# The 50 trips of a written-out loop become hardware loops of two trips: a graph layer with 30 feed-forward steps on one core

## The chip, the core and the metric

One core of a Trainium2 chip. The metric is the device time of one execution in microseconds (us). The kernel uses all engines: TensorE (PE; PEld is its weight load), VectorE (DVE), ScalarE (ACT), GpSimd (POOL) and SyncE (SP), which issues most DMAs.

## The reference

There are 12500 nodes of 256 features and 200000 edges sorted by destination.

```python
xn = _layernorm(x)
support = xn @ gnn_weight
gnn  = relu(segment_sum(support[src] * edge_weight[:, None], dst))
mix  = attention_linear(xn)                # 4 heads, k and v normed, kv summed over all nodes, then wo, bo
x1 = x + gnn + mix
h = _layernorm(x1)
for _ in range(30):                        # lax.scan
    h = h + 0.01 * tanh(h)
    h = h * sigmoid(h)
    h = layernorm(h, ln_w, ln_b)
    h = h @ W.T + b
out = x1 + h
```

## The kernel before

The rows are cut into 100 tiles of 125 rows. There are three stages. Stage A norms x into `xn_d`. Stage B (the `b_trip` function of each engine, 10 passes of 10 tiles, most of them in a hardware loop, `Fori`) sums the attention's kv matrix, and aggregates the messages of the first tiles. Stage F is the rest, and the longest: the 30 feed-forward steps.

Stage F has 5 rounds (`ROUNDS`) of 20 tiles. A round has 10 trips (`TRIPS`), and a trip has 15 slots (`SLOTS`). A slot is one feed-forward step of four tiles, a quad; five quads (`QUADS`) take turns, so a trip is three steps of all five. In a slot PE transposes the next quad (`f_transpose`, L1357 in `quad_transpose`) and multiplies the present one (`f_multiply`, L1365 in `quad_multiply`). ACT does tanh (L747), silu (L757), copies the transposed rows (L770) and norms two or three tiles (L762). DVE does the sum after tanh (L1139), the statistics (L1107, L1112), the shift (L1117) and the low part of a split product (`f_low`, L1152). POOL computes the reciprocal deviation (L494) and norms a tile (L581).

Twelve of 15 slots split the product in three matmuls of a faster type (24 matmuls); the others use 16 slower ones. In rounds 0 to 3 the trips also carry the work of the next round's 20 tiles (flags `g` and `xx` of `f_trip`): POOL gathers source rows (L529, 17 chunks of 128 edges a tile), DVE builds a matrix for each chunk (`hot`, L991), PE sums them (`AGG`, L1252, after a wait for `hot_ready` in L1249), and a few matmuls, copies and loads follow (XB). The last round has none of this, and all 15 slots are split.

Each engine runs its own program. The order of the work is the order in which `f_trip` emits it; engines meet only in semaphores. Every wait in stage F is against a count that follows from the trip number `t`, the round `r` or the trip within the round `u`, as in

```python
n = t * SLOTS + s
pe.wait_ge(S("normed"), n + 1)
pe.wait_ge(S("hot_ready"), j * KC + (c + 1))
```

Before the change `trips_of_f` calls the body 50 times in Python. So each of the 50 trips stands in the program of each engine as its own instructions, and all these counts are constants. In stage B, where the trips are in a `Fori`, the counts are worked out in registers while the program runs, on the engine's own sequencer, and PE's loop starts after one written-out pass.

Of the kernel before, what the change touches and what calls it, by code (L numbers as in the profile page):

```python
# [23 lines left out]
ROUNDS = TILES // ROUND  # L24
SLOTS = 3 * QUADS
TRIPS = STEPS // 3
# [4 lines left out]
LAST_G = G_TRIPS // TRIPS  # L31
# [72 lines left out]
def build(nc, x, src, dst, ew, w_gnn, wq, wk_t, wv_t, wo_t, bo, gk, bk, gv, bv, ln_w, ln_b, wf_t, bf, out):  # L104
# [14 lines left out]
    with ctx:  # L119
# [169 lines left out]
        def trips_of_f(eng, body):  # L289


            for r in range(ROUNDS):
                more = r < ROUNDS - 1
                for u in range(TRIPS):
                    end = u == TRIPS - 1
                    body(r * TRIPS + u, u % 2, r, u, end, more and not (end and r == LAST_G), more, not more and end)

        def splits(t, s, xx):

# [10 lines left out]
        def _(sp):  # L310
# [131 lines left out]
            def f_trip(t, h, r, u, end, g, xx, last):  # L442
# [18 lines left out]
                if end:  # L461
                    for q in range(QUADS):
                        out_store(r, q)

            trips_of_f(sp, f_trip)
            sp.wait_ge(S("out_stored"), 32 * QUADS * ROUNDS)
            sp.wait_ge(S("edges_loaded0"), 48 * (TILES // 2 + 1))
# [4 lines left out]
        def _(pool):  # L472
# [117 lines left out]
            def f_trip(t, h, r, u, end, g, xx, last):  # L590
                for s in range(SLOTS):
# [22 lines left out]
                    if not (last and s + 3 >= SLOTS):  # L614
                        f_rstd(n + 3, (s + 3) % QUADS)

            trips_of_f(pool, f_trip)


        @block.scalar  # L620
        def _(act):
# [165 lines left out]
            def f_trip(t, h, r, u, end, g, xx, last):  # L787
                for s in range(SLOTS):
# [31 lines left out]
                    if g and s == A_TAIL + 2:  # L820
                        g_relu(t * 2 + EARLY_G, xb_use(t, 3))

            trips_of_f(act, f_trip)


# [655 lines left out]
```

## Time and profile before

| what | value |
|---|---|
| time before, median of 3 runs | 4650.79 us (4643.75 to 4659.26) |
| the profiled execution: its own time, its span | 4659.26 us, 4657.4 us |
| PE busy over the span, matmuls | 4163.1 us (89%), 28680 |
| PE weight loads | 3764.2 us (81%), 28680 |
| DVE, ACT, POOL busy | 80%, 76%, 69% |
| instruction fetch, q8 and q14 | 229 packets, 3.75 MB; 165 packets, 1.35 MB |
| granted TensorE clock, mean | 0.976 |

The span runs from the first to the last instruction. A share is a mean over all stages. Stage F fills about four fifths of the span. Instructions of the sequencer (waits, register operations, branches) do not count as busy; they stand in the trace under the engine's name with a q.

### The profile page before, as it was taken

Reading aid. Unit: us, or ns where it says so; the run is one execution under the profiler, and the core shown is the slowest. Engines: PE = TensorE matmul, PEld = TensorE weight load, DVE = VectorE, ACT = ScalarE, POOL = GpSimd, SP = SyncE. Lnnn points to the kernel's source line nnn. Section 1 sums busy time; section 2 is a strip of 40 time slices with the busy share of each in tenths; the row PEclk is TensorE's granted clock in tenths of the full one; section 3 lists DMA queues with packets and bytes.
Section 4 is the critical chain, followed back from the end, with each engine's and each line's share of the span. In section 5 each row is a group of like instructions: output and inputs, shape, how many; then the busy total and the mean of one; then the engine's idle time right before and its main releaser. Section 6 shows DMA issues by size and latency. Waiting matters only on the chain.

```text
span 4657.4 us, 86661 instructions
## 1 busy us (share of the span) xinstructions
PE 4163.1 (89%) x28680; PEld 3764.2 (81%) x28680; DVE 3741.5 (80%) x7288; ACT 3522.3 (76%) x5199; POOL 3219.2 (69%) x3713
## 2 busy tenths in 40 slices
PE   0377777799999999999999999999999999888888
PEld 0244544699999999999999999999999999888888
DVE  4355555688888898888898888889888888888888
ACT  3212211588888888888888888888888889888887
POOL 2445555588888888888888888888888886444444
PEclk9698999899999999999999999999999999999999
DMA  6433333222222232222232222223222221100000
GB/s 202 129 104 105 108 99 107 71 77 77 77 72 77 77 99 72 77 77 77 72 94 82 78 71 78 76 78 93 77 77 78 72 78 54 45 1 1 1 1 23
DMA packets 229800, 351.47 MB, mean 75 GB/s; under 512 B 78161, under 2 KB 168382, under 8 KB 229406
## 3 DMA queue, kind: packets, MB, share of 16 engines
q0 software_dynamic: 82496, 224.47, 16.5%
q1 hardware_dynamic: 142873, 117.94, 8.8%
q8 instruction: 229, 3.75, 0.3%
q10 hardware_dynamic: 4037, 3.95, 0.3%
q14 instruction: 165, 1.35, 0.1%
HBM read 307.30 MB, written 38.91 MB: 74 GB/s over the span
## 4 chain that ended last, share of the span: by engine, by line
PE 65%; DVE 17%; issue 5%; ACT 4%; another core or an unknown queue 4%; POOL 2%; DMA 2%; DVEq 0%; SPq 0%; ACTq 0%; POOLq 0%
PE MM L1365 36%; PE AGG L1252 11%; PE TR L1357 11%; DVE st L1107 4%; DVE T L1139 4%; DVE v_low L1152 4%; PE XB L1264 3%; ACT T L747 3%; PE MM L1288 1%; DVE hot L991 1%; POOL gat L529 1%; DVE k_ss L1008 1%; DVE sh L1117 1%; PE XB L1258 1%
## 5 line engine op out<-in xcount | busy, mean ns | idle before, releaser
L529 POOL DMA_INDIRECT gat<-xn_d,src_cur x1700 | 1691.2, 995 | 685.3 <-issue 443.7
L1365 PE MATMUL MM<-w_high,v_high 128*125 128x256 f32 x5040 | 1464.4, 291 | 0.0
L1365 PE MATMUL MM<-w_low,v_high 128*125 128x256 f32 x5040 | 1416.8, 281 | 0.0
L1365 PE MATMUL MM<-w_high,v_low 128*125 128x256 f32 x5040 | 1415.8, 281 | 0.0
L1139 DVE SCALAR_TENSOR_TENSOR T<-T,MM 125x1024 f32<-125x1024 f32 x725 | 884.4, 1220 | 406.8 <-ACT T L747 403.4
L762 ACT ACTIVATE T<-T,sh,rs 125x256 f32<-125x256 f32 x2102 | 1109.7, 594 | 32.5 <-DVE sh L1117 29.3
L1107 DVE BATCH_NORM_STATS2 st<-T 125x6 f32<-125x512 f32 x1500 | 989.4, 701 | 1.1 <-ACT T L757 1.0
L1252 PE MATMUL AGG<-gat,hot 128*125 128x256 f32 x3400 | 865.4, 386 | 127.4 <-DVE hot L991 65.0
L494 POOL TENSOR_TENSOR rs<-ve,minus_half 125x4 f32<-125x4 f32 x755 | 783.7, 1038 | 230.2 <-DVE ve L1112 218.3
L1365 PEld LDWEIGHTS MM<-w_high,v_high 128*125 128x125 f32 x5040 | 938.8, 186 | 0.0
L1365 PEld LDWEIGHTS MM<-w_low,v_high 128*125 128x125 f32 x5040 | 936.2, 186 | 0.0
L1365 PEld LDWEIGHTS MM<-w_high,v_low 128*125 128x125 f32 x5040 | 935.7, 186 | 0.0
L747 ACT ACTIVATE T<-MM 125x1024 f32<-125x1024 f32 x725 | 740.7, 1022 | 229.2 <-PE MM L1365 226.2
L1357 PE MATMUL TR<-ident,T 125*128 125x125 f32 x6040 | 782.3, 272 | 143.5 <-DVE v_low L1152 118.5
L1357 PEld LDWEIGHTS TR<-ident,T 125*128 125x128 f32 x6040 | 680.9, 141 | 256.1 <-DVE v_low L1152 175.3
L1252 PEld LDWEIGHTS AGG<-gat,hot 128*125 128x125 f32 x3400 | 614.0, 190 | 260.3 <-issue 120.1
L757 ACT ACTIVATE T<-T 125x1024 f32<-125x1024 f32 x750 | 789.5, 1053 | 0.0
L581 POOL TENSOR_SCALAR T<-T,rs,sh 125x256 f32<-125x256 f32 x898 | 499.6, 559 | 374.8 <-DVE sh L1117 355.3
L1152 DVE SCALAR_TENSOR_TENSOR v_low<-TR,v_high 128x1000 fp32r<-128x1000 f32 x630 | 750.2, 1191 | 2.2 <-ACT v_high L770 2.2
L770 ACT ACTIVATE v_high<-TR 128x1000 fp32r<-128x1000 f32 x630 | 631.9, 1003 | 78.7 <-PE TR L1357 62.6
L991 DVE TENSOR_SCALAR hot<-iota_f,d_loc,w_loc 128x125 f32<-128x125 f32 x1700 | 506.0, 349 | 0.0
L1365 PE MATMUL MM<-w_plus,v_full 128*125 128x256 f32 x1920 | 434.3, 379 | 0.0
(176 smaller groups left out, 2963.3 us busy)
## 6 DMA issues: line engine op xcount, KB each, us to landing
gat<-xn_d,src_cur POOLq DMA_INDIRECT x1700
k_x<-xn_d SPq DMA_DIRECT2D x100, 125.0 KB
g_u<-gen_d SPq DMA_DIRECT2D x100, 125.0 KB
g_x<-in_x SPq DMA_DIRECT2D x100, 125.0 KB
a_x<-in_x SPq DMA_DIRECT2D x24, 512.0 KB, 5.5
xn_d<-a_n SPq DMA_DIRECT2D x24, 512.0 KB, 3.9
x_cur<-x_d SPq DMA_DIRECT2D x25, 448.0 KB
out_rows<-x_cur SPq DMA_DIRECT2D x25, 448.0 KB
```

The lines of the kernel that those rows point to most:

```text
L494: pool.tensor_tensor(out_, var, minus_half[0:p, 0:n], ALU.pow).then_inc(S(done), 1)
L529: pool.indirect_dma_start(gat[c][:], None, xn_d, bass.IndirectOffsetOnAxis(ap=src_cur[e][:, c:c + 1], axis=0)).then_inc(S(f"gathered{c}"), 16)
L747: nc.scalar.activation(lane(T, q), product(b), ACT.Tanh).then_inc(S("tanh_done"), 1)
L757: nc.scalar.activation(lane(T, q), lane(T, q), ACT.Silu).then_inc(S("silu_done"), 1)
L762: last = nc.scalar.activation(T[0:R, q * QT + t, :], T[0:R, q * QT + t, :], ACT.Identity, bias=sh[q][0:R, t:t + 1], scale=rs[q][0:R, t:t + 1])
L770: nc.scalar.activation((v_high if split else v_full)[b][:], TR[:, :, 0:4 * R], ACT.Copy, bias=1.0).then_inc(S("transposed_copied"), 1)
L1107: last = v.bn_stats(st[q][0:R, t:t + 2].rearrange("p t k -> p (t k)"), rows_[:, t:t + 2, :].rearrange("p t f -> p f t"))
L1139: v.scalar_tensor_tensor(out=lane(T, q), in0=lane(T, q), scalar=0.01, in1=h, op0=ALU.mult, op1=ALU.add).then_inc(S("u_done"), 1)
L1152: v.scalar_tensor_tensor(out=v_low[b][:], in0=TR[:, :, 0:4 * R], scalar=1.0, in1=v_high[b][:], op0=ALU.add, op1=ALU.subtract).then_inc(S(" ...
L1252: mm(AGG[0:R, 0:D], hot[c][:], gat[c][:], start=c == 0, stop=c == KC - 1).then_inc(S("chunks_multiplied"), 1)
L1357: last = tp(TR[:, t // 2, at:at + R], T[0:R, q * QT + t, h * 128:(h + 1) * 128], ident[0:R, 0:R])
L1365: last = mm(MM[b][0:R, t // 2, t % 2 * D:(t % 2 + 1) * D], rows_, w, start=k == 0, stop=k == len(products) - 1)
```

## The change

The 50 calls become loops of the hardware (`Fori`) whose body is two trips, with the tenth pair of each round behind the loop, because the last trip of a round has other flags. Rounds 0 to 2 stand in an outer loop; rounds 3 and 4 are written out, each with its own inner loop. Each inner loop runs four times. So 12 trips stand in the program instead of 50, and `t`, `u` and (in the first nest) `r` are values in registers. The work, its order, and every count that is waited for are the same.

```diff
-            for r in range(ROUNDS):
+            with eng.Fori(0, LAST_G) as r:
+                with eng.Fori(0, TRIPS // 2 - 1) as u:
+                    for h in range(2):
+                        body(r * TRIPS + u * 2 + h, h, r, u * 2 + h, False, True, True, False)
+                for h in range(2):
+                    body(r * TRIPS + (TRIPS - 2 + h), h, r, TRIPS - 2 + h, h == 1, True, True, False)
+            for r in range(LAST_G, ROUNDS):
                 more = r < ROUNDS - 1
-                for u in range(TRIPS):
-                    end = u == TRIPS - 1
-                    body(r * TRIPS + u, u % 2, r, u, end, more and not (end and r == LAST_G), more, not more and end)
+                with eng.Fori(0, TRIPS // 2 - 1) as u:
+                    for h in range(2):
+                        body(u * 2 + (r * TRIPS + h), h, r, u * 2 + h, False, more, more, False)
+                for h in range(2):
+                    body(r * TRIPS + TRIPS - 2 + h, h, r, TRIPS - 2 + h, h == 1, more and h == 0, more, not more and h == 1)
```

`LAST_G` is 3, `TRIPS` is 10, `ROUNDS` is 5. The arguments of `body` are `t, h, r, u, end, g, xx, last`.

## Rows read from the trace of the kernel before

**Rows 1.** The page: busy us (share) and instructions; fetch queues: packets, MB.
```profile
PE 4163.1 (89%) x28680; PEld 3764.2 (81%) x28680; DVE 3741.5 (80%) x7288; ACT 3522.3 (76%) x5199; POOL 3219.2 (69%) x3713
...
q8 instruction: 229, 3.75, 0.3%
...
q14 instruction: 165, 1.35, 0.1%
```

**Rows 2.** Windows: stretch, us; PE, PEld, DVE, ACT, POOL busy; clock; DMA share; GB/s.
```profile
2125.50:2280.40 154.90, 153.08 (x1098) 143.52 (x1097) 136.03 (x266) 137.17 (x201) 126.61 (x144) 1.00 0.27 76
4250.80:4384.50 133.70, 117.68 (x963) 111.48 (x964) 114.16 (x180) 116.17 (x152) 62.95 (x90) 1.00 0.00 1
```

**Rows 3.** Chain of the last round, in order: start us, us, what.
```profile
4255.94 2.86 PE MM L1365 x24
...
4264.85 2.86 PE MM L1365 x24
```

**Rows 4.** One line's instructions, stage B's loops, 250 to 760 us; ns min/median/max.
```profile
L1323 PEldq COMPARE_BRANCH  x8: 83/215/238, 317.3 to 751.9; - x8
...
L1249 PEldq ALU_OP  x256: 32/32/32, 262.8 to 745.8; - x128
...
L990 DVEq ALU_OP  x272: 40/40/40, 261.9 to 744.4; - x136
```

**Rows 5.** DVE timeline, in stage B's loop and in stage F: start us, us.
```profile
304.91 1.36 DVE L991 TENSOR_SCALAR hot<-iota_f,d_loc,w_loc 128x125 f32<-128x125 f32 x5
...
1022.36 0.85 DVE L991 TENSOR_SCALAR hot<-iota_f,d_loc,w_loc 128x125 f32<-128x125 f32 x3
```

**Rows 6.** PE timeline across a back edge of stage B's loop.
```profile
317.21 2.07 PE L1264 MATMUL XB<-w_agg,xb_t 128*125 128x256 f32 x4 [6.43 <-ACT xb_t L671]
319.07 0.62 PE L1280 MATMUL TR<-ident,k_x 125*128 125x125 f32 x2
```

**Rows 7.** DMA queues, 250 to 750 us, then 1018 to 1020 us.
```profile
q8 instruction: 1, 0.02, 0.0%
...
q8 instruction: 1, 0.02, 3.0%
```

**Rows 8.** Line L514's group, and DMA issues: KB each, us to landing.
```profile
L514 POOL DMA_INDIRECT u_g<-xn_d,u_src x1 | 1.3, 1293 | 9.6 <-DMA u_row<-in_dst 9.6
...
lnb_c<-in_ln_b ACTq DMA_DIRECT2D x2, 0.5 KB, 5.4
...
u_g<-xn_d,u_src POOLq DMA_INDIRECT x1, 4.1
```

**Rows 9.** PE around a trip's end: L1249, the chain, PE's timeline.
```profile
L1249 PEldq EVENT_SEMAPHORE  x2: 51/51/51, 2282.2 to 2282.4; - x2
...
2285.32 0.85 PE TR L1357 x8
...
2290.37 0.81 PE L1357 MATMUL TR<-ident,T 125*128 125x125 f32 x6
```

**Rows 10.** DVE timeline across the same trip's end.
```profile
2285.55 1.22 DVE L1139 SCALAR_TENSOR_TENSOR T<-T,MM 125x1024 f32<-125x1024 f32 x1 [0.34 <-ACT T L747]
...
2286.76 1.32 DVE L1107 BATCH_NORM_STATS2 st<-T 125x6 f32<-125x512 f32 x2
...
2288.20 1.19 DVE L1152 SCALAR_TENSOR_TENSOR v_low<-TR,v_high 128x1000 fp32r<-128x1000 f32 x1
```

**Rows 11.** PE timeline after two pauses of stage B, then windows.
```profile
286.88 1.99 PE L1252 MATMUL AGG<-gat,hot 128*125 128x256 f32 x8 [2.47 <-issue]
...
351.67 3.78 PE L1252 MATMUL AGG<-gat,hot 128*125 128x256 f32 x8 [3.20 <-issue]
...
351.67:355.30 3.63, 3.63 (x9) 2.86 (x10) 1.37 (x4) 1.16 (x4) 0.86 (x1) 0.50 0.15 46
```

**Rows 12.** Waits, 1740 to 3900 us: who for whom, us, times, longest us.
```profile
POOL gat L529 <- issue: 243.3, 906, 2.1
...
PEld TR L1357 <- issue: 5.4, 9, 1.3
```

## The prediction

> **What bounds the kernel now.** I read the page first, then windows of whole trips, the chain, and the instructions around one trip's end. The page gives the means [rows 1]; the windows show that they hide two regimes. Two trips of rounds 0 to 3 take 154.90 us, 77.45 a trip, and PE is busy 153.08 us of them [rows 2]: PE is the bound, with 1% to spare. In the last round two trips take 133.70 us, 66.85 a trip, and PE is busy 117.68 of them [rows 2]. There a ring of waits sets the pace: from one batch of 24 matmuls to the one two slots later the chain takes 4264.85 - 4255.94 = 8.91 us [rows 3], 4.45 a slot, and 15 slots are 66.8 us. In both regimes no time is spent on branches or fetches that any row of stage F shows, apart from small waits put down to issue [rows 12].
>
> **What the change adds and removes.** No matmul, transfer or count changes. Removed are 38 of 50 trips from the program. Added are three things.
>
> *Registers.* Counts that were constants are computed. Stage B does this already. PE has 256 register operations of 32 ns for the waits of L1249 in eight passes, and DVE 272 of 40 ns for 136 chunks, two each [rows 4]. Yet five hot matrices take 1.36 us in that loop and three take 0.85 us in stage F [rows 5]: with 0.34 us for one (an operation outlasts its turn), both are 0.255 us each. So DVE's register work runs under the operation before it. In stage F most DVE and ACT operations are longer than a hot, and PE's sequencer is far ahead (next paragraph). I cost this at nothing; its cover is the operation that runs meanwhile. From above: if two 40 ns operations stayed in the open in each of 750 slots it would be 60 us. The hot rows are nearest, so zero.
>
> *The branches themselves.* A compare-and-branch of PE takes 0.215 us [rows 4]; across a back edge of stage B the transposes start at 319.07 while the matmuls before them end at 319.28 [rows 6]. Nothing is lost there.
>
> *The code at the branch's target.* This is the term that decides. In 250 to 750 us, with PE seven times round its loop of one pass, one packet of instructions came on q8 [rows 7]: a body that small stays with the engine. The new bodies are larger. Two trips are 1098 + 1097 = 2195 matmuls and weight loads [rows 2], without waits and register work. q8 carried 3.75 MB for 57,360 of them [rows 1], 65 bytes each, so a body is over 140 KB, five or more times stage B's. No row shows a branch back over so much. I take it that the code at the loop's head is gone by then, and that PE stops until it has come. DVE, ACT and POOL (266, 201 and 144 operations [rows 2]) may stop too, more likely DVE.
>
> The Trainium skill's page "Runtime: NRT & Kernel Launch" (section on instruction fetch mechanics) says that a taken branch to code outside the engine's small store, 128 KiB on PE and 32 KiB elsewhere, waits for a DMA fetch. It speaks against this change: by it PE, with 140 KB and more, misses at every back edge and the sum is the one below; were only the small loops of the trace to go by, the body might as well stay and the sum would be nothing. No run shows yet which holds.
>
> How long is a miss, L? From below it is the packet alone: 3.0% of 16 engines in 2 us, 0.96 us for 16 KB [rows 7]. From above it is a transfer of 0.5 KB that stood behind others, 5.4 us from issue to landing [rows 8]. Nearest is the single gather of L514: 4.1 us to landing, of which POOL spent 1.3 writing it [rows 8], so 2.8 us, and a fetch's packet is 0.96 longer: L = 3.7 us.
>
> What is covered? At the end of the trip at 2280 PE's sequencer passed its last wait for a chunk at 2282.4, and PE reached the next transposes at 2285.32 [rows 9]: it had 2.9 us of matmuls ahead. From these I take off 0.8 us, by choice, for the loop's register work and the waits behind the branch (32 and 51 ns each [rows 4, 9], with gaps between them): 2.1 us of cover. DVE's side gives the same. Its branch can be passed once the sum of 2285.55 is released; the next statistics start at 2286.76, 1.2 us later; and the low part that follows ends at 2289.39, 0.98 us before the transposes at 2290.37 that need it [rows 9, 10]: 2.2 us. The two run side by side, so the longer counts, not both. A back edge costs L - 2.1 = 1.6 us. PE has 1% to spare, so nothing is caught up.
>
> There are 15 taken back edges of inner loops and 2 of the outer. In rounds 0 to 3 that is 12 + 2 = 14: 14 x 1.6 = 22.4 us. In the last round there are 3; PE idles 0.5 us a slot there, and DVE's body is a third shorter and may stay: L - 2.4 = 1.3 us, 3.9 us. SP misses at outer edges at most, and its loads are issued far ahead: nothing.
>
> Sum: 22.4 + 3.9 = 26.3; for what two or three engines that miss together add to each other I put 3 us more, by choice. 29 us on the profiled execution's 4659.26 is 4688; that one was the slowest of three, 0.2% over the median, so from 4650.79 I forecast **4680 us**, +0.6%.
>
> At the bounds: L = 0.96 costs nothing; L = 5.4 costs 14 x 3.3 + 3 x 3.0 = 55 us. A pause of 2.47 us left PE fast (8 matmuls in 1.99 us); after one of 3.20 us the same 8 took 3.78, and the windows show the clock at 0.50, the 1.2 GHz level [rows 11]. So at L = 5.4 each edge would also pay up to 1.8 us, 31 more: 4737.
>
> **Rivals.**
>
> *Nothing happens* (27%). The code stays, or the fetch comes in the shade of the 2.9 us that PE is ahead. For it: the small loops, and the cover of over 2 us. It decides at L below 2.9 us (14 x 0.8 = 11 us, under 0.3%). Time: 4645 to 4664, most likely 4651.
>
> *The registers are in the open* (10%). Each slot pays 0.08 us on the path, because PE's bound leaves no slack: 60 us besides the 29, 4740. Against it: rows 5. For it: the last round's ring runs through small DVE operations (shift, variance), where there is less to hide under.
>
> *Faster* (6%). Straight code makes the engines fetch 229 and 165 packets [rows 1]; if loops of ACT, POOL and SP stay, part of that traffic is gone, and with it the waits put down to issue at PE's transposes: 5.4 us in 2160 us [rows 12], some 10 us over stage F. POOL's 243.3 us over 906 gathers are 0.27 us each [rows 12], a regular gap that no fetch explains, so I leave them out. 4641 us.
>
> **How the numbers follow.** The forecast (misses that cost 0.8 to 3.3 us an edge) has 57%; its own range is 4664 to 4737. What a measurement tells from no change is about 0.3%, 14 us. Slower: 57 + 10 = 67%. Same: 27%. Faster: 6%. The range from 4643 to 4735 leaves out the worst of the registers, the end of the clock's case and the end of the fast side, some 2 in 10 together.
>
> **What the new profile would show.** PE pauses of 1 to 2 us every 155 us, put down to issue or to an engine that paused itself, and trips between them at 77.5 us; q8 still above 220 packets, as each pass is fetched anew, and q14 below 165 if some bodies stay. If the trips between the edges are longer than 77.5, the registers are the cause. If q8 falls to some 60 packets, the body stays and the forecast's first step is wrong. I would be wrong above all in L, and in how far misses of several engines add up instead of lying side by side.

## The result, and the profile after

| | median us (lowest to highest) | runs |
|---|---|---|
| before | 4644.23 (4629.45 to 4659.26) | 7 |
| after | 4691.23 (4666.44 to 4700.16) | 7 |

The ratio is 1.0089, with a 95% interval of 1.0064 to 1.0114: slower by 47 us between the medians and by 41 by the ratio, whose interval is 30 to 53 us. The profiled execution of after took 4715.59 us (span 4713.7), above all the timed ones. It entered stage F 17.5 us later than the profiled execution of before, behind code that the change does not touch. So stage F is compared by itself: from the start of ACT's tanh of slot 4 (slots counted from 0) in the first trip to the same one of the last trip. It took 3702.7 us before and 3741.4 after, **+38.7 us**. The trace holds 50 such starts, 15 slots apart, and each trip's length is a difference of two of them.

The page of after, to be held against [rows 1]; then one group of its fifth part, and its chain:

```profile
PE 4175.6 (89%) x28680; PEld 3781.5 (80%) x28680; DVE 3741.3 (79%) x7288; ACT 3523.1 (75%) x5199; POOL 3232.2 (69%) x3713
...
q8 instruction: 263, 4.31, 0.4%
...
q14 instruction: 215, 1.76, 0.1%
...
PE 65%; DVE 15%; issue 8%; ACT 4%; another core or an unknown queue 3%; POOL 3%; DMA 2%; DVEq 0%; ACTq 0%; SPq 0%; POOLq 0%
...
L1115 DVE BATCH_NORM_STATS2 st<-T 125x6 f32<-125x512 f32 x1500 | 989.9, 702 | 28.8 <-issue 27.9
```

The program shrank to 12 trips, yet both fetch queues carry more packets than before (229 and 165): each pass fetches its code anew. "Issue" is 8% of the chain. DVE sat idle 27.9 us for it before its statistics, 2 us for each of the 14 edges of rounds 0 to 3.

PE's branches, by line: L292 is the outer loop, L293 the inner loop in it, L300 the inner loops of rounds 3 and 4 (ns min/median/max, then first and last start). Last, the list of PE's waits (us in total, times, longest):

```profile
L292 PEldq COMPARE_BRANCH  x3: 79/4164/5327, 1684.4 to 3258.6; - x3
...
L293 PEldq COMPARE_BRANCH  x12: 83/3828/4582, 1058.0 to 3103.5; - x12
...
L300 PEldq COMPARE_BRANCH  x8: 83/3504/4252, 3414.2 to 4575.0; - x8
...
PE TR L1365 <- issue: 32.3, 16, 3.5
```

A branch that falls through takes 0.08 us. A taken one takes about 4 us, and that is the miss: PE's sequencer stands in the branch until its target has come. PE's transposes then waited for issue in 16 places, 32.3 us together; before, no such wait stands in the list for this line. The waits are shorter than the branches because PE had matmuls queued. The chain at one edge shows how much (start us, us, what):

```profile
1214.52 2.86 PE MM L1373 x24
1217.38 0.86 PE AGG L1260 x4
1218.24 1.93 issue
1220.17 1.05 PE TR L1365 x8
```

The branch began at 1215.68 and ended at 1219.54. PE's queued matmuls ran out at 1218.24, 2.56 us after its start. From the branch's end to the transposes at 1220.17 are another 0.63 us of register work and waits. So the cover was 2.56 - 0.63 = 1.93 us, and the pause 1.93.

The clock is the second part. Windows behind three edges (stretch, us; PE, PEld, DVE, ACT, POOL busy; clock; DMA share; GB/s), and the chain across the third and the second of them:

```profile
1220.20:1223.00 2.80, 2.80 (x25) 2.80 (x26) 1.41 (x3) 1.75 (x3) 2.22 (x3) 1.00 0.25 61
1690.50:1692.40 1.90, 1.87 (x9) 1.90 (x10) 0.00 (x0) 0.00 (x0) 1.06 (x1) 0.50 1.03 314
...
3421.00:3423.50 2.50, 2.50 (x15) 2.50 (x13) 2.44 (x6) 1.52 (x4) 1.38 (x2) 0.53 0.00 0
```
```profile
3416.79 2.17 issue
3418.97 1.05 PE TR L1365 x8
3420.01 4.37 PE MM L1373 x24
```
```profile
1687.01 3.52 issue
1690.53 1.90 PE TR L1365 x8
1692.43 4.58 PE MM L1373 x24
```

After a pause of 1.93 us PE went on at 1.00, the 2.4 GHz level. After one of 3.52 us it ran at 0.50, the 1.2 GHz level: 8 transposes and 24 matmuls took 6.48 us instead of 3.91, 2.6 us lost besides the pause. After one of 2.17 us the drop came late, and cost 4.37 - 2.86 = 1.5 us. By the starts of matmuls two other edges (1850, 4174 us) lost some 1.5 us each in this way. Together the clock is about 7 of the 38.7 us. The length of the pause alone does not decide it: after 2.58 us, the longest pause at an inner edge (1060.6), PE went on at full speed, and after 2.05 us, at 4172.3, it did not.

### The profile page after: what moved, and what is told of

Read it like the earlier page. It is cut to its first block, busy times and chain, and to the rows that moved or that the text cites. A ratio compares the mean times of both kernels' runs of the same rounds, so it can differ in the third digit from the quotient of the medians.

```text
span 4713.7 us, 94631 instructions
## 1 busy us (share of the span) xinstructions
PE 4175.6 (89%) x28680; PEld 3781.5 (80%) x28680; DVE 3741.3 (79%) x7288; ACT 3523.1 (75%) x5199; POOL 3232.2 (69%) x3713
## 4 chain that ended last, share of the span: by engine, by line
PE 65%; DVE 15%; issue 8%; ACT 4%; another core or an unknown queue 3%; POOL 3%; DMA 2%; DVEq 0%; ACTq 0%; SPq 0%; POOLq 0%
PE MM L1373 35%; PE AGG L1260 12%; PE TR L1365 11%; DVE st L1115 4%; DVE T L1147 4%; PE XB L1272 3%; DVE v_low L1160 3%; ACT T L755 3%; PE MM L1296 2%; POOL gat L537 2%; DVE hot L999 1%; PE XB L1266 1%; DMA a_x<-in_x 1%; DVE sh L1125 1%
## 5 line engine op out<-in xcount | busy, mean ns | idle before, releaser
L1115 DVE BATCH_NORM_STATS2 st<-T 125x6 f32<-125x512 f32 x1500 | 989.9, 702 | 28.8 <-issue 27.9
L1260 PE MATMUL AGG<-gat,hot 128*125 128x256 f32 x3400 | 876.8, 390 | 136.5 <-DVE hot L999 74.2
```

The lines of the kernel that those rows point to most:

```text
L1115: last = v.bn_stats(st[q][0:R, t:t + 2].rearrange("p t k -> p (t k)"), rows_[:, t:t + 2, :].rearrange("p t f -> p f t"))
L1260: mm(AGG[0:R, 0:D], hot[c][:], gat[c][:], start=c == 0, stop=c == KC - 1).then_inc(S("chunks_multiplied"), 1)
```

## The experiments

All change `trips_of_f` only. Kernels of one group shared the runs of before: e1 to e4 with 4652.37 us (18 runs), e5 to e8 with 4660.93 (23), e9 to e12 with 4651.65 (17). F is the extra length of stage F in the one profiled execution of each, in us over before's 3702.7. In the columns after it, F is taken apart by trips, each against the same trip of before: the 12 trips that begin at a taken inner edge in rounds 0 to 3; the two outer edges, each with the two trips before and the two behind it; the last round. What is missing, under 3 us, lies elsewhere. F is one execution's. It stands up to 8 us from the difference of the medians and up to 12 from the ratio, so differences of a few us between two kernels are read from edges and trips, not from F.

| kernel | median us | ratio (95%) | F | inner | outer | last |
|---|---|---|---|---|---|---|
| after | 4691.23 | 1.0089 (1.0064 to 1.0114) | +38.7 | 25.8 | 7.6 | 5.2 |
| e1 hints on all loops | 4672.31 | 1.0041 (1.0026 to 1.0055) | +13.5 | -3.9 | 14.2 | 1.4 |
| e2 outer loop only | 4659.31 | 1.0011 (0.9999 to 1.0024) | +6.8 | -1.7 | 9.3 | -0.2 |
| e3 PE alone loops | 4695.28 | 1.0082 (1.0068 to 1.0095) | +40.7 | 26.0 | 7.4 | 7.1 |
| e4 the four others loop | 4673.44 | 1.0033 (1.0021 to 1.0046) | +20.2 | 11.4 | 8.2 | -0.1 |
| e5 inner loops only | 4692.41 | 1.0089 (1.0065 to 1.0113) | +36.4 | 28.8 | -0.1 | 7.0 |
| e6 the same, with hints | 4668.00 | 1.0024 (1.0009 to 1.0040) | +3.4 | -3.3 | 1.5 | 2.9 |
| e7 DVE alone loops | 4678.37 | 1.0041 (1.0025 to 1.0058) | +20.9 | 14.5 | 8.3 | 0.0 |
| e8 POOL alone loops | 4674.71 | 1.0031 (1.0015 to 1.0046) | +16.9 | 10.3 | 6.3 | -0.2 |
| e9 hints on PE alone | 4676.34 | 1.0048 (1.0030 to 1.0067) | +22.5 | 14.0 | 7.3 | 1.3 |
| e10 hints on the others | 4706.43 | 1.0125 (1.0106 to 1.0143) | +47.1 | 23.8 | 17.0 | 3.7 |
| e11 four trips a pass | 4672.42 | 1.0059 (1.0037 to 1.0080) | +15.8 | 6.7 (4 edges) | 7.9 | 2.9 |
| e12 ACT alone loops | 4649.65 | 1.0001 (0.9986 to 1.0016) | +1.5 | 0.0 | 1.5 | -0.1 |

### e1: a branch hint on every loop

```diff
+            def loop(n):
+                return nc.Fori(0, n, engines=OrderedEngineSet([eng.engine]), hint_back_edge=True)
-                with eng.Fori(0, TRIPS // 2 - 1) as u:
+                with loop(TRIPS // 2 - 1) as u:
```

The same stands for the outer loop. In the trace it is one more instruction on each engine, at the head of each pass; PE's, for the outer and the inner loop:

```profile
L296 PEldq BRANCH_PREFETCH_HINT  x3: 45/45/55, 873.8 to 2443.4; - x3
L297 PEldq BRANCH_PREFETCH_HINT  x12: 31/36/36, 874.1 to 2909.7; - x12
```

> All loops of stage F on all engines announce their back edge at the head of each pass, so that the code at the loop's head can be fetched while the pass runs. Nothing else differs from the changed kernel; the registers and branches stay. Theory 1 (missing code at the branch): PE's taken branches fall from about 4 us to under 0.5 us, and the time comes back to the kernel before within 0.2% (up to 10 us over it). Theory 2 (register work in the open): the time stays about 40 us (0.9%) over the kernel before. Theory 3 (the nest of loops disturbs something else, such as the order of loads): it stays too, and PE's branches are short.

PE's branches in e1, outer and inner loop; its waits; and DVE's chain at the first outer edge:

```profile
L296 PEldq COMPARE_BRANCH  x3: 88/5176/5557, 1654.4 to 3221.5; - x3
L297 PEldq COMPARE_BRANCH  x12: 88/357/383, 1032.6 to 3064.7; - x12
```
```profile
PE TR L1369 <- issue: 7.6, 2, 4.0
```
```profile
1659.75 2.76 issue
...
1662.72 2.67 issue
1665.39 0.04 DVEq L297
```

At inner edges the branch fell from 3.8 to 0.36 us and the loss was gone. With register work and branches as before, this shows the fetch to be the cause. At the two outer edges the hint did nothing: 5.2 and 5.6 us. The outer loop's hint stands at the head of its pass (873.8), 780 us ahead of its branch, and the inner one's follow it (874.1); that they take its place is my reading, not tested. There DVE stopped twice, in the outer loop's code and at the entry of the hinted inner loop, and the two trips that begin at outer edges cost 11.4 us, against 7.5 in after.

The other 2.7 us of the column's 14.2 lie before the outer edges. The trip behind an inner loop's exit was 1.2 to 1.3 us longer than in before in rounds 0 to 2, and in after it was not longer by more than 0.5. ACT paused there, some 13 us behind its exit; e1, then the same place in after:

```profile
1513.87 1.58 ACT L774 ACTIVATE T<-T,sh,rs 125x256 f32<-125x256 f32 x3 [1.33 <-issue]
...
1544.38 1.57 ACT L770 ACTIVATE T<-T,sh,rs 125x256 f32<-125x256 f32 x3
```

So a hint also costs something, once a loop. Over the exits of rounds 0 to 3 it is 4.1 us in e1 and in e10, which hints all engines but PE, and nothing in e9, which hints PE alone. That the code fetched for the loop's head takes the place of the code behind the loop would explain it, and was not tested. With this, e1 stayed 13.5 us over before in F and 20 in the median, where at most 10 were expected.

### e2: the outer loop alone, ten trips written out in it

```diff
             with eng.Fori(0, LAST_G) as r:
-                with eng.Fori(0, TRIPS // 2 - 1) as u:
-                    for h in range(2):
-                        body(r * TRIPS + u * 2 + h, h, r, u * 2 + h, False, True, True, False)
+                for u in range(TRIPS):
+                    body(r * TRIPS + u, u % 2, r, u, u == TRIPS - 1, True, True, False)
```

The last two rounds are written out.

> Only the outer loop over rounds 0 to 2 is kept; its ten trips are written out in the body, and rounds 3 and 4 are written out with constants as before. So 30 of 50 trips count in registers, and there are 2 taken back edges in place of 17. Theory 1: two misses of 4 to 5 us on PE, 4 to 10 us over the kernel before, 0.1 to 0.2%. Theory 2: three fifths of the 41 us, 25 us or 0.5%.

30 trips still compute their counts in registers, and away from the edges each is between 0.7 us shorter and 0.2 us longer than the same trip of before. So the registers cost nothing. The loss that is left, 9.3 us, stands at the two taken edges.

### e3 and e4: who pays

```diff
+            (trips_looped if eng.engine == mybir.EngineType.PE else trips_written)(eng, body)
```

In e3 PE alone has the loops, and the other engines the old 50 trips; e4 has `!=`.

> PE alone has the loops; the other four engines run written-out trips with constants, as before. PE's 17 taken back edges stay. Theory 1 with PE's misses as the cause: 20 to 35 us over the kernel before, since each miss of 4 us is 1 to 2 us longer than what PE has ahead. If DVE's and POOL's misses are the cause: under 10 us. Theory 2 with PE's registers: 20 us or more, but spread over all trips, not at the edges.

> The reverse: DVE, ACT, POOL and SP have the loops, PE runs written-out trips. Theory 1 with PE's misses as the cause: at most 15 us over the kernel before (DVE's and POOL's misses of about 2.7 us are 0.5 us longer than DVE's cover of 2.2 us, at 14 edges). If the misses of the others count as much as PE's: 20 us or more. Theory 2 with registers on DVE, ACT and POOL: 30 us or more, in all trips.

PE's misses alone give the whole loss, those of the other four half of it: 40.7 and 20.2, while all together give 38.7. They do not add up. At an edge the longest pause counts. Both came out above what was expected (20 to 35, at most 15). In e3, 5 half-speed stretches behind edges are part of it; in e4, the misses of DVE and POOL count for more than was thought (see e7, e8).

### e5 and e6: no outer loop

```diff
-            with eng.Fori(0, LAST_G) as r:
-                (the nest above)
-            for r in range(LAST_G, ROUNDS):
+            for r in range(ROUNDS):
```

Every round has its own inner loop; e6 adds the hint of e1.

> The outer loop is gone: each of the five rounds has its own inner loop of four passes, without hints; 15 taken edges are left, all of them inner ones. Theory (each taken edge pays for its own miss, the two outer ones more than the inner ones): the changed kernel lost about 0.9% or 41 us; the two outer edges had taken branches of 5.33 and 4.16 us on PE and pauses of 3.9 and 2.7 us, so 6 to 7 us go away and +34 us is left, a ratio of 1.0073. Rival (the outer edges, where all engines miss at once, carry most of the loss): +15 us or less, 1.0033. Second rival (the outer loop's register r costs too): trips without an edge get shorter than 77.5 us.

> As the kernel with no outer loop, with the branch hint on all five inner loops of each engine. Theory (the loss is the misses and nothing else, and the hint takes away those of inner edges, but not those of outer ones): the taken branches of PE take some 0.35 us, no PE pause at any edge, and the time is that of the kernel before, within 5 us (0.999 to 1.001). Rival (the hinted kernel's +19 us came mainly from something that the hint itself adds, such as fetches ahead that disturb other transfers, or from the registers): +10 to +15 us stays, 1.002 to 1.003, with trips over 77.5 us.

e5 won 2.3 us in F where 6 to 7 were expected, and nothing in the ratio. The loss of the outer edges did go (7.6 to -0.1 us). But the inner edges lost 28.8 us instead of 25.8, and the last round 7.0 instead of 5.2. The largest piece is the first edge of round 2, with 4.4 us against 1.4 in after; its chain:

```profile
2601.94 2.94 issue
2604.88 1.38 PE TR L1359 x8
2606.26 4.06 PE MM L1367 x24
```

PE's branch took 4.97 us there (3.80 in after), and PE then ran at half speed for a while, which is 1.5 us. Half speed came behind 5 edges in e5. So most of what the outer edges gave back was lost again, by the clock and by one long miss.

ACT, whose code had stayed in all inner loops of after, now missed at the three edges of round 2 (2.5 to 3.6 us), and POOL missed in round 3. The instructions are the same, only their place in the program differs. ACT's misses lay beside PE's: the third edge of round 2 cost 2.4 us with a miss of ACT, and 2.5 in after without one.

e6 has the hint's small branches in four rounds, but in round 2 PE's still took 2.2 to 3.2 us. It is the best looped kernel, though not within the 5 us of before that were expected. Its interval starts at +0.09%, and F accounts for 3.4 us of the 7 between the medians; the rest is open. The five trips behind the exits of the hinted loops are 6.1 us longer than in before (1.5 in e5), more than F as a whole. ACT 3 us behind its exit from round 1's loop:

```profile
2293.92 1.00 ACT L773 ACTIVATE v_high<-TR 128x1000 fp32r<-128x1000 f32 x1 [2.21 <-issue]
```

### e7, e8 and e12: one engine at a time

The edit is e3's line with `DVE`, `Pool` and `Activation`.

> DVE alone runs the loops (as changed, outer loop too); the four other engines have their trips written out. The kernel in which DVE, ACT, POOL and SP all loop lost 0.33% (15 us in the same runs). Theory (DVE's miss of 2.7 to 3.0 us at the edges of rounds 0 to 3 is what that kernel paid for, since PE waits for DVE's matrices and low parts): DVE alone gives most of it, +10 to +15 us, 1.002 to 1.003. Rival (it is POOL's miss, which delays the norm): DVE alone gives under 5 us, 1.001 or less. By the forecast's cover of 2.2 us it would be 14 x 0.6 = 8 us.

> POOL alone runs the loops; the other engines have their trips written out. Theory (DVE sets the loss of the others, POOL's miss of 2.5 us in rounds 0 to 2 lies under the slack of the gathers and the norm): +0 to +4 us, at most 1.001. Rival (POOL sets it): +10 to +15 us, 1.002 to 1.003.

> ACT alone runs the loops. In the changed kernel ACT paused for code at outer edges only. Theory (a loss needs a miss; register work and branches cost nothing): the inner edges cost nothing, trips at 77.5 us, the two outer edges up to 3 us each; stage F +2 to +6 us, ratio 1.001 or less. Rival (any engine that loops costs some 17 to 21 us, as DVE and POOL did, through register work at each edge, not through the miss): +15 us or more, 1.003.

PE's waits for one row of each: e7, then e8.

```profile
PE TR L1378 <- DVE v_low L1173: 132.7, 202, 3.9
```
```profile
PE TR L1378 <- POOL T L602: 16.9, 20, 1.9
```

In before these were 118.5 us (186 times, longest 1.3) and 2.8 us (7 times). I expected POOL's miss to lie under slack, since POOL is busy 69%. It doesn't: its share of the norm comes late, and PE's transposes wait for it. POOL's timeline at an inner edge of round 0, and at one of round 3 (start us, us, what, idle before):

```profile
1212.88 1.04 POOL L515 TENSOR_TENSOR rs<-ve,minus_half 125x4 f32<-125x4 f32 x1
1216.25 1.06 POOL L550 DMA_INDIRECT gat<-xn_d,src_cur  x1 [2.32 <-issue]
...
3558.76 1.03 POOL L515 TENSOR_TENSOR rs<-ve,minus_half 125x4 f32<-125x4 f32 x1
3560.09 1.13 POOL L550 DMA_INDIRECT gat<-xn_d,src_cur  x1 [0.30 <-issue]
```

In rounds 0 to 2 POOL missed (2.5 to 2.7 us), and each of the 9 edges cost 1.1 to 1.2 us. In round 3 it did not, and its three edges cost 0.0. ACT did not miss at inner edges, and they cost 0.0 as well. These are the controls: loop, registers and branch cost nothing on these engines; without a miss there is no loss.

DVE's timeline at an edge in e7:

```profile
1194.60 1.22 DVE L1160 SCALAR_TENSOR_TENSOR T<-T,MM 125x1024 f32<-125x1024 f32 x1 [0.38 <-ACT T L768]
1195.73 0.15 DVE L1138 SCALAR_TENSOR_TENSOR sh<-st,rs 125x4 f32<-125x4 f32 x1
1197.68 1.31 DVE L1128 BATCH_NORM_STATS2 st<-T 125x6 f32<-125x512 f32 x2 [1.79 <-issue]
```

The next register instruction ran at 1197.45, 2.7 us after the branch's end. The statistics came 1.8 us late, and this edge cost 0.6 us. Over the 12 inner edges of e7 the miss was 2.7 to 3.5 us, 3.15 in the mean, the statistics came 2.2 us late and an edge cost 1.2: 1.0 us was absorbed before PE's transposes. So F is 20.9 us, above the 10 to 15 expected.

### e9 and e10: hints on one side

The hint's condition is `eng.engine == mybir.EngineType.PE`, then `!=`.

> The changed kernel with the branch hint on PE's loops alone; DVE, ACT, POOL and SP keep their misses. Theory (misses of several engines at one edge lie side by side, and the longest pause counts): PE's inner edges cost nothing now, and what DVE's or POOL's miss costs alone comes to light: stage F is 20 to 24 us longer than before, as with DVE alone (+20.9) or the four others (+20.2); ratio 1.004 to 1.005. Rival (the misses of the engines share the changed kernel's loss of +38.7 us between them, and PE alone lost 40.7, so the others' share in it is nothing): +5 us or less.

> The mirror of it: the hint on the loops of DVE, ACT, POOL and SP, none on PE's. Side by side: PE's miss is the longest and sets the edge, nothing is won: stage F +38 to +41 us over before, ratio 1.008 to 1.009. If the misses added to each other, half of the loss would go: +20 us, 1.0045.

PE's inner branches and DVE's waits in e9, then PE's inner branches in e10:

```profile
L297 PEldq COMPARE_BRANCH  x12: 87/357/383, 1034.2 to 3072.0; - x12
```
```profile
DVE st L1119 <- issue: 27.4, 14, 2.5
```
```profile
L297 PEldq COMPARE_BRANCH  x12: 76/3688/4087, 1046.1 to 3100.0; - x12
```

With PE's misses taken away, those of the others come to light at 14.0 us for 12 edges, as in e7. With theirs taken away and PE's left, nothing is won at inner edges (23.8). This is the test of "side by side" by subtraction. In F e10 is 8.4 us slower than after, where next to no change was expected. The trips that begin at outer edges cost 14.3 us instead of 7.5: PE paused twice at each, with 3.9 and 2.2 us from matmul to matmul at the first, 3.3 and 3.2 at the second. The trips behind the loops' exits add 4.7, as in e1; the other edges cost somewhat less.

### e11: four trips in a pass

```diff
-                with eng.Fori(0, TRIPS // 2 - 1) as u:
-                    for h in range(2):
-                        body(r * TRIPS + u * 2 + h, h, r, u * 2 + h, False, True, True, False)
+                with eng.Fori(0, 2) as u:
+                    for h in range(4):
+                        body(r * TRIPS + u * 4 + h, h % 2, r, u * 4 + h, False, True, True, False)
```

> The inner loop has four trips in its body and runs twice, without hints: 5 taken inner edges and 2 outer ones instead of 15 and 2. Theory (the loss goes by the number of taken edges, 38.7 us over 17 of them, 2.3 us each): 7 x 2.3 = 16 us in stage F, ratio 1.0035, and trips within the body of 77.5 us. Rival (the code that a trip reads is what costs, however seldom it branches, or a longer body makes each miss dearer): +25 us or more.

F is +15.8 us, at 16 forecast: five inner edges of 1.2 to 1.9 us and two outer ones of 7.9 together. In rounds 0 to 3 no trip within a body was more than 0.3 us longer than in before. The loss goes by taken edges. ACT, with twice the code, now missed at inner edges (idle in brackets; DVE's statistics waited for ACT in turn):

```profile
1187.97 1.02 ACT L755 ACTIVATE T<-MM 125x1024 f32<-125x1024 f32 x1 [0.32 <-PE MM L1373]
1190.99 1.06 ACT L765 ACTIVATE T<-T 125x1024 f32<-125x1024 f32 x1 [1.99 <-DVE T L1147]
```

The row names DVE, but DVE's operation was long done; ACT's next register instruction came 2.7 us after its branch. The timed ratio says more, 17 to 37 us; so the profiled execution's figure is rather low, and the proportion holds roughly. The rival of +25 us or more lies within this interval; what speaks against it is where the loss stands, not its size.

## Why the prediction was right, and where its sizes were off

It was forecast at +29 us, from misses at taken edges. It was 30 to 53 us by the runs and 38.7 in stage F. The mechanism was right and its size a quarter too small. The forecast of 4680 us is nearer to the 4691 than its terms deserve: the 3 us put in by choice have no counterpart, and they cover part of what the other terms lack.

| term | forecast | measured |
|---|---|---|
| 12 inner edges, rounds 0 to 3 | 12 x 1.6 = 19.2 | 25.8, 2.15 each |
| 2 outer edges | 2 x 1.6 = 3.2 | 7.6 |
| 3 edges of the last round | 3.9 | 5.2 |
| several engines together | 3 | none seen at inner edges |
| registers, branches | 0 | 0 |

**The code at the branch's target.** Right: no body as large as PE's stayed. Counting the trace's records, a pass of PE has 2433 in rounds 0 to 3 and 2076 in the last, and PE missed in both. A store of 2048 instructions for PE and 512 for the others is what the Trainium skill gives ("Runtime: NRT & Kernel Launch", instruction fetch mechanics); that fits PE. By that figure alone DVE with 400 and POOL with 294 should not have missed; they did, and the measurement decides. The Trainium skill also says there that the store is two pages of 256 instructions; if so, the place counts. The runs agree: bodies of 220 or fewer (DVE, ACT and POOL in the last round) never missed, those of 400 always did, and those of 294 did in one place and not in another (POOL in rounds 0 to 2 against round 3 of after; ACT in round 2 of e5 alone). That bodies straddle page borders in just this way was not measured.

**The length of a miss.** 3.7 us forecast, from a gather's landing and a packet. Measured: 3.3 to 4.6 us in PE's inner branches, near 4.0 in the middle, 4.2 and 5.3 at outer ones. At inner edges DVE took 2.7 to 3.5 us and POOL 2.4 to 2.9.

**The cover.** 2.1 us forecast, 1.93 at the edge shown: PE was 2.56 us ahead instead of 2.9, and the work behind the branch took 0.63, not 0.8. Over the 12 inner edges of rounds 0 to 3 the branch took 4.0 us in the mean and PE paused 2.0 (1.35 to 2.58), where I had 1.6. So this term was mis-sized by 0.4 us an edge, 0.3 of it by L.

**The clock.** I counted it only at the upper bound, L = 5.4, as in before a pause of 2.47 us had left PE fast [rows 11]. In after, pauses of 3.52 and even of 2.17 us were followed by half speed at 4 of 17 edges, 7 us in all; 3 of them are in the 25.8. One pause that left PE fast was no proof for pauses near it.

**The outer edges.** I gave them the inner edges' price. What is different there is the traffic. DMA share, GB/s and queues of after in 7 us around an inner edge, then in 11 us around the outer edge at 1684:

```profile
DMA packets 232, 0.33 MB, mean 47 GB/s; under 512 B 162, under 2 KB 163, under 8 KB 227
...
q8 instruction: 2, 0.03, 1.9%
```
```profile
DMA  9999999999999799999999999999999689632653
...
DMA packets 2761, 3.08 MB, mean 280 GB/s; under 512 B 213, under 2 KB 2625, under 8 KB 2752
...
q1 hardware_dynamic: 2562, 2.47, 73.4%
...
q8 instruction: 2, 0.03, 1.2%
```

The round's output is being written, and the DMA engines are over 90% busy: the fetch shares them with that. PE's branch took 5.33 us here, against 3.86 at the quiet edge. But the second outer edge speaks against traffic as the whole cause. In its branch's window the DMA engines were as busy, and the branch took 4.16 us, no longer than at inner edges (up to 4.58):

```profile
2474.00:2478.00 4.00, 2.07 (x15) 1.61 (x13) 3.97 (x8) 1.90 (x3) 2.66 (x4) 1.00 0.94 278
```

ACT, which stayed at inner edges, missed at both outer ones as well. No run moved the output away from the edge; the cause is argued, not shown.

**Side by side.** Right, shown by e3, e4, e9 and e10. The 3 us for engines missing together should not have been added at inner edges.

**DVE's side.** The cover of 2.2 us was nearly right, and came from two parts, 1.2 and 0.98. In e7 the mean miss of 3.15 us made the statistics 2.2 late, so the first part was 0.9; an edge cost 1.2, so the second was 1.0. What the expectation of e7 had too small was L: with 2.7 to 3.0 us it gave 0.6 us an edge. I also left POOL out, and it carries 1.1 us an edge by itself. Neither changed the sum, as PE's pause is longer.

**The rivals.** Nothing happens: fell with L above 2.9 us. Registers in the open: fell by e2, e8 and e12, and by the trips between the edges of after, which are as long as those of before. Faster: fell; of the two queues, q8 rose to 263 and q14 to 215, where I had said that q14 would fall below 165 if some bodies stay. ACT's stayed and it rose nevertheless; with hints, in e1, it was 108.

No version here beats before. e12 equals it, but loops one engine only; e6 loops all of them at +0.24%.

## What to carry to other kernels

A loop's back edge is free only while its body stays with the engine; otherwise price it as one miss (here 2.4 to 5.6 us) less what the engine has queued, for the engine with the longest pause, and allow for half speed where PE then stands about 2 us or more. If the program must shrink, make few and long passes, hint the innermost loops, and look at each engine in the trace at the edge and also behind the loop's exit, where hinted loops lost up to 2.3 us. The place of the code alone can turn a hit into a miss. That large transfers near the edge make a miss longer was not shown. In a pipeline that is bound by one engine and coupled tightly, an engine that is busy 69% has no 2.5 us to spare.

## What was not expected of the hardware

- The same 294 instructions of POOL missed in rounds 0 to 2 and stayed in round 3, and missed there too when e5 moved them. ACT's stayed in all inner loops of after and missed in round 2 of e5.
- A hint on an inner loop took PE's branch from 3.8 to 0.36 us; on the loop around it, it did nothing (5.2 and 5.6 us), and engines then paused twice at the outer edge (DVE 2.76 and 2.67 us).
- Hints on DVE, ACT and POOL made the trip behind the loop's exit longer, by up to 1.3 us in e1 and 2.3 in e6, with pauses of ACT of 1.33 and 2.21 us that after does not have.
- Some trips were 0.6 us shorter than in before (76.9 instead of 77.5): 6 of the 12 at inner edges of e1, but also 4 in rounds 0 to 2 of e2, which has no inner loop. So it is not the hint; no run explains it.
- The clock fell after a pause of 2.17 us, only from 1.05 us behind it (e.g. 24 matmuls in 4.37 us after transposes at full speed), and stayed up after one of 2.47 us [rows 11] and one of 2.58 us in after itself.
